# Reordering one pipeline step of a two-stream windowed-attention stage: the first exponentials between the head-out copies, q and k ahead of P on SyncE, and TensorE's third and fourth scores ahead of the second values

## The chip, the cores and the metric

One core of one Trainium2 chip runs the whole program. The time is the device time in microseconds of one execution. The kernel before took 4911.67 us (median of 3 runs, 4908.47 to 4913.42).

## The reference, cut to what matters

The program computes a modulated block: a layer norm, an RWKV-like recurrence over 4096 tokens of two batches, and then two layers of windowed attention with a gated MLP. The change touches only those two layers. With the window length 128, 8 heads of 64, and T = 4096:

```python
def _layer(x, wqkv, qs, ksc, wo, lg, lb, w1, b1, w2, b2):
    h = shift_token(x)
    q, k, v = split(h @ wqkv)                      # 8 heads of 64
    q, k = rotary_xpos(l2norm(q) * qs, l2norm(k) * ksc)
    o = local_attention(q, k, v)                   # own window of 128 keys and the one before
    x = x + o @ wo
    h = layernorm(shift_token(x)) * lg + lb
    a, g = split(h @ w1 + b1)
    return x + (a * gelu(g)) @ w2 + b2

for l in range(2):
    x = _layer(x, ...)
return x_attn + gb * x
```

All tensors are float32.

## The kernel before

Five stages run one after the other: setup, mix, scan, gate and local. `local_stage` holds the two layers. A window is 128 tokens; a layer has NW = 32 windows, and both layers are walked in one loop over u = 0 to 63 (u < 32 is the first layer). Two streams s = 0, 1 are the two batch elements. The work is cut into steps called `half(s, u, w, l)`, with w = u % 2. Such a step does the score and softmax part of stream s, window u, and at the same time the second part (values, output projection, layer norm, MLP) of the other stream o = 1 - s, whose window `um` was scored one step earlier. It also projects q, k and v of the window u + 1 of its own stream s. There are 128 steps; all but the first have the second part (`mlp=True`).

Each engine has its own list of these parts, in an order written out by hand; engines run their lists in order and meet by semaphores. The order on each engine in one step before the change:

- TensorE (PE): values 0 and 1 of o (`values`, L2516, needs group 0 of the turned P), scores 0 and 1 of s (`scores`, L2498, needs the turned q and k), in the second layer the two transposes of `turn_out` (L2567), values 2 and 3 of o (needs group 1 of P), scores 2 and 3 of s, `project_out` of o (L2524, needs both head-out copies), then k projection, mean, v projection, variance, q projection (L2462, L2529, L2533), `hidden` (L2551) and `out` (L2559).
- Scores of head pair 0 and 2 are written to banks B and C of stream s, those of pair 1 and 3 to bank A of s and bank A of o. So scores 2 wait until `row_max` 0 has read its banks, and scores 3 wait until `row_max` 1 has read its own (the wait for `mx` with `after(n, 2)`).
- VectorE (DVE): `add_out`, `norm_k`, `row_max` 0 (L2182: mask and maximum, then L2189: the negative bias `nb`), in the second layer `scale_out`, `row_max` 1, 2, `inverse_sums` 0, `row_max` 3, `attended` (L2206, needs `project_out`), `inverse_sums` 1, `turn_k` (L2156), the four `turn_p` (L2198) with other parts between, and the q work and `gate` of the MLP.
- ScalarE (ACT): `carry`, `head_out` 0 and 1 (L2363: copy of the values' result out of PSUM; number 1 needs values 2 and 3), `exponent` 0 to 3 (L2354, needs `nb` of its pair), `square_dev`, `copy_v`, and the rest.
- GpSimd (POOL): `rotate_k` (L2015 to L2020), `normalise` 0, `join_x1`, `normalise` 1 and 2, and the rest.
- SyncE (SP) moves P and q, k through scratch memory to turn them: `write_p` 0 (L1919), `write_qk` of the other stream (L1898), `write_p` 1, `read_p` 0 (L1931, four transfers), `read_qk` (L1909, four transfers), `read_p` 1. A read waits for the landing of its write. What is read in one step is used by PE in the next.

Of the kernel before, what the change touches and what calls it, by code (L numbers as in the profile page):

```python
# [1745 lines left out]
def local_stage(nc, persist, a, T):  # L1746
# [14 lines left out]
    with ExitStack() as ctx:  # L1761
# [92 lines left out]
        with nc.Block() as block:  # L1854
            @block.sync
            def _(sp):
# [30 lines left out]
                def write_qk(s, u):  # L1887

                    sp.wait_ge(S["q_turned"][s].sem, S["q_turned"][s].after(u))
                    sp.sem_inc(sems["free"], 1)  # L1890
                    sp.wait_ge(S["k_turned"][s].sem, S["k_turned"][s].after(u))
                    sp.sem_inc(sems["free"], 1)
                    sp.wait_ge(S["qkT"][s].sem, S["qkT"][s].after(u, 1))
                    sp.sem_inc(sems["free"], 1)
                    if not isinstance(u, int) or u > 1:
                        sp.wait_ge(S["kT"][s].sem, S["kT"][s].after(u - 1))
                        sp.sem_inc(sems["free"], 1)
                    sp.dma_start(a["qkz"][s], qk[s][:].rearrange("p j y h t -> p (j y h t)")).then_inc(S["qk_out"][s].sem, 16)  # L1898

                def read_qk(s, u, w):  # L1900

                    sp.wait_ge(S["qk_out"][s].sem, S["qk_out"][s].after(u))
                    sp.sem_inc(sems["free"], 1)
                    sp.wait_ge(Q["sc"][s].sem, Q["sc"][s].after(u * NHP - 1))
                    sp.sem_inc(sems["free"], 1)
                    turned = a["qkz"][s].rearrange("(i c) (j n) -> j c i n", i=BL, j=BL)
                    cur = (2, 1)[w] * BL
                    for j in range(BL):
                        sp.dma_start(qkT[s][32 * j:32 * j + 32, cur:cur + BL].rearrange("p i y h t -> p i (y h t)"),  # L1909
                                     turned[j]).then_inc(S["qkT"][s].sem, 16)  # L1910

                def write_p(s, u, g):

                    sp.wait_ge(Q["p_turned"][s].sem, Q["p_turned"][s].after(u * NHP + 2 * g + 1))
                    sp.sem_inc(sems["free"], 1)
                    sp.wait_ge(H[g]["pT"][s].sem, H[g]["pT"][s].after(u, 1))
                    sp.sem_inc(sems["free"], 1)
                    n = 32 * NHP
                    sp.dma_start(bass.AP(a["pz"].tensor, (s * 2 + g) * AREA + (BL - 1) * 32 * n,  # L1919
                                         [[(2 * BL + 1) * n, P], [32 * n, NR], [1, n]]),  # L1920
                                 pb[s][:, g].rearrange("p r h t -> p (r h t)")).then_inc(H[g]["p_out"][s].sem, 16)
# [28 lines left out]
                def half(s, u, w, l, mlp=True):  # L1950
                    o = 1 - s
                    um, wm_ = partner(s, u, w)
                    un, wn = um + 1, 1 - wm_
                    fin = not isinstance(u, int) or u > 0
                    if fin and not layer(u - 1, l):
                        store(s, u - 1, 0)
                    if at(s, u, 1, NW):
                        sp.wait_ge(S["w2_ps"][1].sem, S["w2_ps"][1].after(NW - 1))
                        sp.dma_start(w2[:], a["w2"][1]).then_inc(sems["w2"], 16)
                    if s == 1 and within(u + 2):  # L1960
                        load_rot(u + 2, w, layer(u + 2, l))
                    if mlp and within(um + 2):
                        if isinstance(um, int) and um + 2 == NW:
                            sp.wait_ge(sems["zero"], 16 * NB)
                        load_window(o, um + 2, wm_, layer(um + 2, l))
                    if mlp and layer(um, l):
                        load_xa(o, um)
                    if at(s, u, 0, NW):
                        sp.wait_ge(S["wo_ps"][1].sem, S["wo_ps"][1].after(NW - 1))
                        sp.dma_start(wo[:], a["wo"][1]).then_inc(sems["wo"], 16)  # L1970
                    write_p(s, u, 0)
                    if within(un):
                        write_qk(o, un)
                    write_p(s, u, 1)
                    read_p(s, u, 0)
                    if within(un):
                        read_qk(o, un, wn)
                    read_p(s, u, 1)
                    if fin and layer(u - 1, l):
                        store(s, u - 1, 1)  # L1980
                    if at(s, u, 1, NW - 2):
                        sp.wait_ge(S["q_ps"][1].sem, S["q_ps"][1].after(NW - 1))
                        sp.dma_start(wqkv[:], a["wqkv"][1]).then_inc(sems["wqkv"], 16)
                    if at(s, u, 0, NW):
                        sp.wait_ge(M["w1_ps"][1].sem, M["w1_ps"][1].after(3 * NW - 1))
                        sp.dma_start(w1[:], a["w1s"]).then_inc(sems["w1"], 16)
# [326 lines left out]
            def _(act):  # L2313
# [96 lines left out]
                def half(s, u, w, l, mlp=True):  # L2410
                    o = 1 - s
                    um, wm_ = partner(s, u, w)
                    un, wn = um + 1, 1 - wm_
                    if mlp:
                        carry(o, um, wm_)
                        head_out(o, um, 0)
                        head_out(o, um, 1)
                    exponent(s, u, 0)
                    exponent(s, u, 1)
                    exponent(s, u, 2)  # L2420
                    exponent(s, u, 3)
                    if mlp:
                        square_dev(o, um)
                    if within(un):
                        copy_v(o, un, wn)
                    if within(u + 1):
                        square_k(s, u + 1)
                    if mlp:
                        inverse_std(o, um)
                    if within(u + 1):  # L2430
                        square_q(s, u + 1)
                    if mlp:
                        gelu(o, um, 0, layer(um, l))
                        gelu(o, um, 1, layer(um, l))
                        gelu(o, um, 2, layer(um, l))
                        act.preload_act_table_set(LN_EXP)
                    if within(u + 1):
                        inverse_norms(s, u + 1)
                    if w == 0:
                        copy_k(s, u)  # L2440
# [13 lines left out]
            def _(pe):  # L2454
# [126 lines left out]
                def half(s, u, w, l, mlp=True):  # L2581
                    o = 1 - s
                    um, wm_ = partner(s, u, w)
                    fin = not isinstance(u, int) or u > 0
                    drained = within(um + 1)
                    if mlp:
                        values(o, um, wm_, 0, layer(um, l))
                        values(o, um, wm_, 1, layer(um, l))
                    scores(s, u, w, 0)
                    scores(s, u, w, 1)  # L2590
                    if fin and layer(u - 1, l):
                        turn_out(s, u - 1)
                    if mlp:
                        values(o, um, wm_, 2, layer(um, l))
                        values(o, um, wm_, 3, layer(um, l))
                    scores(s, u, w, 2)
                    scores(s, u, w, 3)
                    if mlp:
                        reloaded("wo", o, um)
                        project_out(o, um)  # L2600
                    if within(u + 1):
                        reloaded("wqkv", s, u + 1)
                        project(s, u + 1, 1 - w, 1)
                    if mlp:
                        mean(o, um)
                    if within(u + 1):
                        project(s, u + 1, 1 - w, 2)
                    if mlp:
                        variance(o, um)
                    if within(u + 1):  # L2610
                        project(s, u + 1, 1 - w, 0)
                    if mlp:
                        reloaded("w1", o, um)
                        hidden(o, um, 0, drained, u)
                        hidden(o, um, 1, drained)
                        hidden(o, um, 2, drained)
                        reloaded("w2", o, um)
                        out(o, um, 0)
                        out(o, um, 1)
                        out(o, um, 2)  # L2620
# [146 lines left out]
```

## Time and profile before

| what | value |
|---|---|
| median of the runs | 4911.67 us |
| the profiled execution | 4915.73 us, its span 4913.9 us |
| PE busy | 4346.3 us (88%) |
| DVE busy | 3295.8 us (67%) |
| ACT busy | 2920.9 us (59%) |
| POOL busy | 2290.3 us (47%) |
| granted TensorE clock, mean | 0.956 |
| local stage | from about 2316 us to the end |
| one step in it | 20.0 us where nothing is late |

An instruction's start is counted from the start of the span. A step begins where PE starts values 0. Groups of matmuls are merged in the rows of the timeline: one row gives the first start and the time until the last one's modelled end. Matmuls overlap, so a group's modelled end lies a little behind the start of the next.

### The profile page before, as it was taken

To read this page: it belongs to the slowest core of one execution; us is meant where nothing else is said; L and a number is where in the kernel's file an instruction comes from. 1 tells how busy PE (TensorE), PEld (TensorE's weight loads), DVE (VectorE), ACT (ScalarE), POOL (GpSimd) and SP (SyncE) were. 2 spreads that over 40 slices of the span, in tenths; PEclk is the share of its full clock that TensorE was granted. 3 is DMA by queue.
4 is the path that set the end of the run, shared out by engine and by line. 5 is a ranking of instruction groups with operands and counts; after the bars stand their busy time and mean duration, and the time that the engine had idled before them with its cause. 6 is when DMAs were issued, how large, how long until landed. Compare 5 with 4: busy or idle time off the path is not lost. (4 is left out here: it accounts for less than half of the span.)

```text
span 4913.9 us, 281580 instructions
## 1 busy us (share of the span) xinstructions
PE 4346.3 (88%) x114072; PEld 3665.2 (75%) x114072; DVE 3295.8 (67%) x10277; ACT 2920.9 (59%) x8550; POOL 2290.3 (47%) x3196
## 2 busy tenths in 40 slices
PE   7888888678888888665999999999999999999998
PEld 6888888668888888653777777777777777777776
DVE  4666666578888888474666666666666666666664
ACT  5777777534444444253666666666666666666665
POOL 1222222257777777302444445444445555555553
PEclk8999999879999999787999999999999999999999
DMA  3334343467777777595666666666676667676665
GB/s 88 88 94 97 90 94 95 103 147 163 164 167 163 164 166 163 143 296 160 153 156 156 154 154 152 151 152 155 162 176 159 160 163 164 161 162 161 158 158 121
DMA packets 1454099, 728.62 MB, mean 148 GB/s; under 512 B 676624, under 2 KB 1398288, under 8 KB 1452816
## 3 DMA queue, kind: packets, MB, share of 16 engines
q1 hardware_dynamic: 1402448, 652.89, 57.6%
q10 hardware_dynamic: 51392, 73.02, 5.1%
q14 instruction: 188, 1.54, 0.1%
q8 instruction: 71, 1.16, 0.1%
HBM read 410.48 MB, written 315.15 MB: 148 GB/s over the span
## 5 line engine op out<-in xcount | busy, mean ns | idle before, releaser
L2354 ACT ACTIVATE l_prob<-l_prob,l_nb,l_rq 128x160 f32<-128x160 f32 x1024 | 518.4, 509 | 14.3 <-DVE l_nb L2189 14.3
L2015 POOL TENSOR_TENSOR l_k<-l_kn,l_tab 128x512 f32<-128x512 f32 x128 | 162.1, 1267 | 613.2 <-DVE l_kn L2163 613.2
L2031 POOL TENSOR_TENSOR l_prob<-l_prob,l_rinv 128x320 f32<-128x320 f32 x512 | 362.8, 719 | 76.3 <-DVE l_rinv L2171 76.1
L2559 PE MATMUL lD<-l_hid,w 128*128 128x128 f32 x3072 | 363.9, 275 | 0.0
L2559 PEld LDWEIGHTS lD<-l_hid,w 128*128 128x128 f32 x3072 | 353.3, 192 | 0.0
L2551 PEld LDWEIGHTS lA<-l_hn,w 128*128 128x128 f32 x2048 | 243.1, 195 | 110.3 <-POOL l_hn L2049 61.1
L2198 DVE STREAM_TRANSPOSE l_pb<-l_prob 128x320 f32<-128x320 f32 x512 | 250.6, 498 | 104.1 <-POOL l_prob L2031 104.1
L2025 POOL TENSOR_TENSOR l_qr<-l_q 128x512 f32<-128x512 f32 x128 | 162.4, 1269 | 329.0 <-DVE l_q L2127 329.0
L1097 POOL TENSOR_TENSOR sc_aqx<-sc_late,sc_headmask 128x256 f32<-128x256 f32 x256 | 172.1, 672 | 278.3 <-PE sc_Y L1190 275.0
L1173 PE MATMUL sc_AB<-sc_aq,sc_bkx 32*32 32x32 f32 x16384 | 258.6, 198 | 39.9 <-POOL sc_bkx L1097 29.7
L497 POOL TENSOR_TENSOR rk<-rk,bkraw 128x256 f32<-128x256 f32 x64 | 54.6, 872 | 477.8 <-DVE bkraw L383 477.8
L2551 PE MATMUL lA<-l_hn,w 128*128 128x128 f32 x2048 | 266.3, 284 | 12.1 <-POOL l_hn L2049 5.6
L2524 PE MATMUL lD<-l_oT,wo 128*128 128x128 f32 x2048 | 264.5, 283 | 0.1
L2524 PEld LDWEIGHTS lD<-l_oT,wo 128*128 128x128 f32 x2048 | 240.1, 193 | 32.7 <-ACT l_oT L2363 30.5
L2462 PE MATMUL lB<-wqkv,l_h 128*128 128x512 f32 x512 | 244.4, 600 | 21.9 <-POOL l_mean_w L2072 21.5
L1115 POOL TENSOR_TENSOR sc_bkT<-sc_tok,sc_headmask 128x128 f32<-128x128 f32 x512 | 257.0, 522 | 0.0
L2551 PE MATMUL lB<-l_hn,w 128*128 128x128 f32 x2048 | 252.0, 277 | 0.0
L1173 PEld LDWEIGHTS sc_AB<-sc_aq,sc_bkx 32*32 32x32 f32 x16384 | 214.5, 108 | 41.9 <-issue 40.9
L2363 ACT COPY l_oT<-lB 128x256 f32<-128x256 f32 x128 | 47.6, 372 | 330.7 <-PE lB L2516 330.7
L2551 PEld LDWEIGHTS lB<-l_hn,w 128*128 128x128 f32 x2048 | 241.7, 194 | 0.0
L2462 PE MATMUL lC<-wqkv,l_h 128*128 128x512 f32 x512 | 241.6, 594 | 0.0
L2462 PE MATMUL lA<-wqkv,l_h 128*128 128x512 f32 x512 | 240.9, 593 | 0.0
(273 smaller groups left out, 13217.1 us busy)
## 6 DMA issues: line engine op xcount, KB each, us to landing
l_pT<-scratch_pz SPq DMA_DIRECT2D x1024, 128.0 KB, 3.7
scratch_pz<-l_pb SPq DMA_DIRECT2D x256, 320.0 KB, 3.0
scratch_qkz<-l_qk SPq DMA_DIRECT2D x128, 512.0 KB, 3.2
l_qkT<-scratch_qkz SPq DMA_DIRECT2D x512, 128.0 KB, 3.8
scratch_cm<-cm SPq DMA_DIRECT2D x64, 512.0 KB, 4.1
sc_early<-scratch_cm ACTq DMA_DIRECT2D x59, 512.0 KB
scratch_tok<-vt SPq DMA_DIRECT2D x512, 48.0 KB, 1.8
scratch_part<-sc_att SPq DMA_DIRECT2D x64, 384.0 KB
```

Of the source, the lines that this page charges most:

```text
L1097: return nc.gpsimd.tensor_tensor(dst[:], src.unsqueeze(2).broadcast_to([P, 2 * BG, HQ, CH]), headmask[:].unsqueeze(1).unsqueeze(3).broadca ...
L1115: last = nc.gpsimd.tensor_tensor(bkT[c % 2][:, b * BG:(b + 1) * BG], tok[k][:, c, b, 1:3].rearrange("p x g i -> p (x g) i").unsqueeze(2) . ...
L1173: last = mm(AB_ps[c][at, (x * BG + q) * QH:(x * BG + q + 1) * QH], bkx[c][at, 2 * q + x].rearrange("p h t -> p (h t)"), aq[c][at, q], star ...
L2015: tt(k1[s][:], kn[s][:], wide(2, slice(0, DH)), ALU.mult)
L2025: tt(qr[s][:], q1[s][:], q2[s][:], ALU.add).then_inc(S["qr"][s].sem, 1)
L2031: tt(prob[s][:, pair], prob[s][:, pair], rinv[s][:, pair].unsqueeze(2).broadcast_to([P, 2, SPAN]), ALU.mult).then_inc(Q["pn"][s].sem, 1)
L2198: nc.vector.transpose(pb[s][:, g, :, at:at + 2].rearrange("p r h t -> p h r t"), prob[s][:, 2 * hp:2 * hp + 2].rearrange("p h (r k) -> p h ...
L2354: last_ = nc.scalar.activation(prob[s][:, h], prob[s][:, h], ACT.Exp, scale=rq8[s][:, h:h + 1], bias=nb[s][:, h:h + 1], accum_out=sums[s][ ...
L2462: last_ = mm(bank[s][j][:], h[:, k * P:(k + 1) * P], wqkv[:, k, j * INNER:(j + 1) * INNER], start=(k == 0), stop=(k == CC - 1))
L2524: last_ = mm(bank[s][3][:, m * P:(m + 1) * P], wo[:, k, m * P:(m + 1) * P], oT[s][:, k], start=(k == 0), stop=(k == NHP - 1))
L2551: last_ = mm(bank[s][j][0:MW, at:at + P], w1[:, k, tile * MW:(tile + 1) * MW], hn[s][:, k], start=(k == 0), stop=(k == CC - 1))
L2559: last_ = mm(bank[s][3][:, c * P:(c + 1) * P], w2[:, m, c * P:(c + 1) * P], hid[s][:, m], start=(c == 0 and m == 0), stop=(c == CC - 1 and ...
```

## The change

Three lists are reordered; nothing is added or removed. On ACT, the first exponentials go between the two head-out copies. On SP, `write_qk` goes ahead of `write_p` 0, and `read_qk` ahead of `read_p` 0. On PE, scores 2 and 3 go ahead of values 2 and 3.

```diff
@@ sync, half
-                    write_p(s, u, 0)
                     if within(un):
                         write_qk(o, un)
+                    write_p(s, u, 0)
                     write_p(s, u, 1)
-                    read_p(s, u, 0)
                     if within(un):
                         read_qk(o, un, wn)
+                    read_p(s, u, 0)
                     read_p(s, u, 1)
@@ scalar, half
                     if mlp:
                         carry(o, um, wm_)
                         head_out(o, um, 0)
+                    exponent(s, u, 0)
+                    if mlp:
                         head_out(o, um, 1)
-                    exponent(s, u, 0)
                     exponent(s, u, 1)
@@ tensor, half
                     scores(s, u, w, 1)
                     if fin and layer(u - 1, l):
                         turn_out(s, u - 1)
+                    scores(s, u, w, 2)
+                    scores(s, u, w, 3)
                     if mlp:
                         values(o, um, wm_, 2, layer(um, l))
                         values(o, um, wm_, 3, layer(um, l))
-                    scores(s, u, w, 2)
-                    scores(s, u, w, 3)
                     if mlp:
                         reloaded("wo", o, um)
                         project_out(o, um)
```

## Rows read from the trace of the kernel before

**Rows 1.** Waits, 3000 to 4800 us (89 steps): who waited, for what, total, times, longest.
```profile
PEld lB L2516 <- DMA l_pT<-scratch_pz: 77.2, 89, 1.7
PEld lD L2524 <- ACT l_oT L2363: 21.1, 84, 0.3
PE lB L2498 <- DMA l_qkT<-scratch_qkz: 16.9, 15, 1.9
```
**Rows 2.** Timeline of PE, a first-layer step: start, length, operation, count [idle before].
```profile
3126.49 1.09 PE L2516 MATMUL lD<-l_pT,l_V 128*64 128x128 f32 x16
3127.82 0.49 PE L2498 MATMUL lA<-l_qkT 64*32 64x160 f32 x16
3129.39 1.09 PE L2516 MATMUL lB<-l_pT,l_V 128*64 128x128 f32 x16 [1.08 <-DMA l_pT<-scratch_pz]
3131.12 2.05 PE L2524 MATMUL lD<-l_oT,wo 128*128 128x128 f32 x16
```
**Rows 3.** Timeline of ACT, the same step: the second head-out copy.
```profile
3130.53 0.37 ACT L2363 COPY l_oT<-lB 128x256 f32<-128x256 f32 x1 [2.52 <-PE lB L2516]
```
**Rows 4.** Windows: stretch, length, busy PE, PEld, DVE, ACT, POOL, clock, DMA, GB/s.
```profile
3131.20:3146.40 15.20, 15.20 (x100) 11.92 (x100) 10.00 (x35) 11.30 (x32) 7.03 (x10) 1.00 0.65 169
3614.00:3617.40 3.40, 1.26 (x40) 0.87 (x42) 1.64 (x13) 0.34 (x1) 3.09 (x4) 1.00 1.10 292
3617.40:3620.80 3.40, 3.40 (x50) 2.48 (x46) 1.37 (x12) 2.20 (x8) 1.28 (x2) 0.50 0.99 392
```
**Rows 5.** Timeline of DVE: turn_k; bias of pair 0 and maximum of pair 1.
```profile
3113.39 0.69 DVE L2156 STREAM_TRANSPOSE l_qk<-l_kr 128x512 f32<-128x512 f32 x1
...
3128.74 0.43 DVE L2189 TENSOR_TENSOR l_nb<-l_mx,l_nrq 128x2 f32<-128x2 f32 x1
...
3129.59 0.08 DVE L2182 DVE_READ_ACCUMULATOR2_ANT l_mx<- 128x1 f32 x1
3129.70 0.16 DVE L2189 TENSOR_TENSOR l_nb<-l_mx,l_nrq 128x2 f32<-128x2 f32 x1
```
**Rows 6.** Timeline of POOL, the same step.
```profile
3127.89 1.27 POOL L2015 TENSOR_TENSOR l_k<-l_kn,l_tab 128x512 f32<-128x512 f32 x1 [5.35 <-DVE l_kn L2163]
```
**Rows 7.** Timeline of 3660.5 to 3664 us: maximum of pair 1, then scores 3.
```profile
3661.35 0.08 DVE L2182 DVE_READ_ACCUMULATOR2_ANT l_mx<- 128x1 f32 x1
...
3661.58 0.51 PE L2498 MATMUL lA<-l_qkT 64*32 64x160 f32 x16
```
**Rows 8.** Timeline of PE, a second-layer step.
```profile
4223.18 0.51 PE L2498 MATMUL lA<-l_qkT 64*32 64x160 f32 x16
4223.61 0.44 PE L2567 MATMUL lD<-ident,l_hout 128*128 128x128 f32 x2
4224.55 1.09 PE L2516 MATMUL lB<-l_pT,l_V 128*64 128x128 f32 x16 [0.49 <-DMA l_pT<-scratch_pz]
```
**Rows 9.** Timeline of DVE, the same second-layer step: maximum of pair 1.
```profile
4225.21 0.08 DVE L2182 DVE_READ_ACCUMULATOR2_ANT l_mx<- 128x1 f32 x1
```
**Rows 10.** Lines L2206 and L2567 over the whole span: durations, first and last start.
```profile
L2206 DVE TENSOR_TENSOR l_x<-lD,l_h x128: 424/425/427, 2327.7 to 4893.7; 128x256 f32<-128x256 f32 x128
L2567 PE MATMUL lD<-ident,l_hout x128: 272/300/331, 3638.9 to 4910.1; 128*128 128x128 f32 x128
```
**Rows 11.** Timeline of SP's queue, a first-layer step.
```profile
3116.66 0.34 SPq L1898 DMA_DIRECT2D scratch_qkz<-l_qk  x1
3117.72 0.36 SPq L1919 DMA_DIRECT2D scratch_pz<-l_pb  x1
3118.72 2.30 SPq L1931 DMA_DIRECT2D l_pT<-scratch_pz  x4
3121.21 1.74 SPq L1909 DMA_DIRECT2D l_qkT<-scratch_qkz  x4
3123.13 1.79 SPq L1931 DMA_DIRECT2D l_pT<-scratch_pz  x4
```
**Rows 12.** Line L1909, 3121.2 to 3123 us: from issue to landing.
```profile
DMA to landing us min/median/max: 3.5/3.9/4.1
```

## The prediction

> **What bounds the kernel now.** I read the page first: the local stage fills the second half of the span, and PE is its busiest engine. The view of waits then says which waits of PE are real. In 89 steps the loads of values 2 wait for the landing of P's group 1 in every one of them, 77.2 us; the output projection waits 0.25 us each for the second head-out copy [rows 1]. The timeline of one step puts these in order. PE starts values 0 at 3126.49, ends scores 1 at 3127.82 + 0.49 = 3128.31, is idle 1.08 us for the DMA, starts values 2 at 3129.39 and the output projection at 3131.12 [rows 2]. That copy starts 1.14 us behind values 2 and takes 0.37 us [rows 3]: 3129.39 + 1.14 + 0.37 = 3130.90, and the projection starts 0.22 us later. So scores 2 and 3 now run in the shadow of that copy and cost nothing. From the projection to the end of the step PE has no gap: 15.20 of 15.20 us busy [rows 4]. The step is therefore one chain: projection, dense PE work, values 0 and 1, scores 0 and 1, a wait, values 2, copy, projection. The wait before values 2 is its only slack of any size, and everything after it moves with the start of values 2.
>
> **PE: scores 2 and 3 ahead of values 2.** The work is the same, but its place is not. Scores 3 overwrite the banks that the maximum of pair 1 reads, so they wait for `row_max` 1, and PE takes its list in order, so values 2, the copy and the projection queue behind that wait. In the first-layer step the maximum of pair 1 ends at 3129.59 + 0.08 = 3129.67 [rows 5]. From such an end to scores 3 the trace of before has one case where PE waited for it: 3661.35 + 0.08 = 3661.43, scores 3 at 3661.58, 0.15 us [rows 7]. From scores of that form to the next work on PE is 4223.61 - 4223.18 = 0.43 us [rows 8]. Values 2 would start at 3129.67 + 0.15 + 0.43 = 3130.25 instead of 3129.39: +0.86 us. The same sum in the second layer, where `scale_out` stands on DVE ahead of `row_max` 1: 4225.21 + 0.08 + 0.15 + 0.43 = 4225.87 instead of 4224.55 [rows 8, 9]: +1.32 us. The neighbouring steps give 0.93 and 1.27 by the same working; I take 0.90 and 1.30.
> Behind values 2 the chain keeps its length: the 1.14 us, the copy and the 0.22 us; only that scores 2 and 3 no longer fill it, which leaves PE idle there about 0.7 us. The shift of values 2 is thus the shift of the step.
> The count: L2206 runs 128 times, once for each second part, the last of them in the closing part, which the change leaves alone: 127 steps. L2567 runs 128 times at two a step, 64, of which two are in the closing part: 62 steps with the longer DVE queue, 65 without [rows 10]. 65 x 0.90 + 62 x 1.30 = 58.5 + 80.6 = 139 us.
>
> Why `row_max` 1 is late has a term of its own. DVE's bias of pair 0 took 0.43 us, the one after it, of the same form, 0.16 [rows 5]; the first ended at 3129.17, where POOL's L2015 ended (3127.89 + 1.27 = 3129.16) [rows 6]. The Trainium skill (SBUF — State Buffer, Who interferes with whom) has the rule for it: a VectorE instruction with two inputs in SBUF and a GpSimd one that reads SBUF exclude each other, and the second to issue blocks for the whole of the first. By the rule the 0.43 stays as long as L2015 starts first; without it the bias would cost 0.16, and the sum would be 127 x 0.27 = 34 us less. The change moves neither instruction against the other, so I keep 0.43, and keep the 34 us as the lower bound of the term.
>
> **ACT: exponentials 0 between the copies.** They can start when the bias of pair 0 is there, 3129.17, and last two activations of 0.51 us by start to start, until about 3130.3. The second copy, then due at 3130.25 + 1.14 = 3131.39, finds ACT free 1.1 us before. Cost 0. They gain 0 too: the exponentials' users, `inverse_sums` 1 and the P turns, stand on DVE behind `attended`, which needs the projection. If values 2 did start at 3129.39 as before, the copy due at 3130.53 would still be clear of them, by 0.2 us.
>
> **SP: q and k first.** `write_qk` needs `turn_k`, done at 3113.39 + 0.69 = 3114.08 [rows 5], and SP is then at the end of the window load that stands before it. It goes out at about 3114.5 instead of 3116.66 [rows 11] and lands before `write_p` 1, so `read_qk` starts at 3118.2, right behind `write_p` 1 (3117.72 + 0.36), where SP now idles until 3118.72 [rows 11]. Then four q, k reads to 3120.0, P's group 0 to about 3122.4, group 1 to 3124.3 instead of 3124.92. What each queue move does:
> - q and k land about 3 us sooner. Scores waited for them in 15 of 89 steps, 16.9 us [rows 1], by 127/89 that is 24 us that can go.
> - P's group 0 is behind them now. Its last read goes out at about 3122.0, where it used to be before 3118.72 + 2.30 = 3121.0, and lands 3.5 to 4.1 us later (the q and k reads in that place have it so [rows 12]): 3125.5 to 3126.1, and values 0 want it at 3126.49 [rows 2]. In a usual step this is in time by 0.4 to 1.0 us. In the 15 of 89 steps where DMAs ran late it is not, and PE will wait at values 0 for what it waited for at scores 0. The two cancel within 0 to 24 us either way; I take 0 and keep -24 and +24.
> - P's group 1 lands 0.6 us sooner, which would be worth 0.6 us a step in the old order. Now values 2 wait for DVE, and this gain is hidden.
>
> **Sum.** 139 + 0 + 0 = 139 us on the profiled execution's 4915.73 (span 4913.9 and 1.8 around it): 5055. That execution is 4.1 above the median, so the median comes to 4911.7 + 139 = 5051.
>
> **The rivals.**
> - A, the forecast: PE's new wait for `row_max` 1. With bounds -34 and -24, +24, about 5000 to 5078.
> - B, faster: the DMA is the loop's real clock. P's group 1 lands 0.6 to 0.9 us sooner and scores 2 and 3 fill the time until then, so the step shortens by up to 0.6: 127 x 0.6 = 76 us, 4835. For it: the DMA wait stands in all 89 steps. Against: scores 3 must be out before the landing, that is, the maximum of pair 1 must end by 3129.39 - 0.6 - 0.43 - 0.15 = 3128.2, and it ends at 3129.67, 1.5 us late. It decides for B only if DVE reaches that maximum before 3128.2.
> - C, P's group 0 becomes late: the reads of 0.4 us slack slip to a wait at values 0 in most steps, 0.4 us each: 139 + 51 = 190 us, 5102. For it: the slack is thin. Against: the whole burst starts 0.5 us earlier.
> - D, absorbed: some slack between projection and values 0 swallows part of the shift; half of it would give 4912 + 70 = 4982. Against: the 15.20 of 15.20 us [rows 4].
> - E, the clock: at 3614.0 to 3617.4 PE was busy 1.26 of 3.40 us and the clock granted in the next 3.4 us was 0.50 (1.2 GHz) [rows 4]. With the new order a step has three idle pieces close together, 0.5, 0.5 and 0.7 us, but some 2.1 of 3.4 us stay busy. A stretch of 3.4 us at half the clock loses 1.7 us at most; in one step of three that is 42 x 1.7 = 71 us on top of A: 5122. The Trainium skill (TensorE: Matmul & The Clock Gate, A second HAM failure mode: psum-queue depth-cycling) says that a TensorE which idles briefly and often between groups of matmuls, as it cycles through PSUM banks, can swing between its two clocks. By that rule this new order is a candidate for E; the trace shows such a fall only once in the steady stage, after much more idling, and speaks against it.
>
> **How the numbers follow.** A 0.77, B 0.05, C 0.09, D 0.05, E 0.04. The predicted time is A's, 5051. Range 5005 to 5095: A without its lowest corner, and the near part of C. A measurement of this kernel tells 0.2%, about 10 us, from no change. Faster is B, 0.05; the same is the far end of D, 0.02; slower the rest, 0.93.
>
> **What would show it.** Right: in the profile after, the DMA wait before values 2 is gone; scores 3 start 0.15 us behind the maximum of pair 1; values 2 start some 3.8 us behind values 0 in the first layer and 4.1 in the second (2.90 before in the first); the projection waits 0.6 to 0.7 us for the copy; steps last 20.9 and 21.3 us. q and k landings no longer appear as waits of scores. Wrong: a DMA wait still ahead of values 2 (B), a wait of L2516's lD loads for P in most steps (C), steps of 20.0 us with idle moved elsewhere (D), granted clock below 1.00 inside the local stage (E).

## The result and the profile after

The changed kernel took 5024.31 us (median of 4 runs, 5023.56 to 5029.4) against 4910.07 us (4 runs): a ratio of 1.0235, 95% interval 1.0218 to 1.0251, about 115 us slower. Forecast were 5051 us, in a range of 5005 to 5095, and slower with 0.93. The profiled span grew from 4913.9 to 5021.7 us.

The waits of the changed kernel, 3000 to 4800 us, about 85 steps (columns as in rows 1). TensorE's lines have moved by one: values are L2517, scores L2499, the projection L2525.
```profile
PE lA L2499 <- DVE l_mx L2182: 55.1, 85, 1.2
PE lB L2499 <- DVE l_mx L2182: 23.7, 69, 0.6
PEld lD L2525 <- ACT l_oT L2363: 59.9, 84, 0.7
PE lD L2525 <- ACT l_oT L2363: 40.2, 85, 0.6
PE lD L2517 <- DMA l_pT<-scratch_pz: 8.5, 12, 1.9
```
The wait of values 2 for P is gone. In [rows 1] their weight loads waited for it in 89 of 89 steps, 77.2 us; as idle time of PE the same view of before has less:
```profile
PE lB L2516 <- DMA l_pT<-scratch_pz: 53.4, 82, 1.3
```
In the changed kernel scores 2 (the lB row) and scores 3 (lA) wait for VectorE's maxima, and the projection (L2525) waits for the copy, now as an idle PE and not only as a held weight load. Values 0 (the lD row of L2517) wait for P in 12 steps, which they did not before; scores no longer wait for q and k at all.

PE in a first-layer step of the changed kernel:
```profile
3193.23 1.09 PE L2517 MATMUL lD<-l_pT,l_V 128*64 128x128 f32 x16
3194.62 0.51 PE L2499 MATMUL lA<-l_qkT 64*32 64x160 f32 x16
3196.55 0.51 PE L2499 MATMUL lA<-l_qkT 64*32 64x160 f32 x16 [0.46 <-DVE l_mx L2182]
3196.99 1.09 PE L2517 MATMUL lB<-l_pT,l_V 128*64 128x128 f32 x16
3198.56 2.05 PE L2525 MATMUL lD<-l_oT,wo 128*128 128x128 f32 x16 [0.47 <-ACT l_oT L2363]
```
VectorE in that step, the bias of pair 0 and the end of the maximum of pair 1, and ScalarE's second copy:
```profile
3195.47 0.44 DVE L2189 TENSOR_TENSOR l_nb<-l_mx,l_nrq 128x2 f32<-128x2 f32 x1
...
3196.33 0.08 DVE L2182 DVE_READ_ACCUMULATOR2_ANT l_mx<- 128x1 f32 x1
```
```profile
3198.13 0.37 ACT L2363 COPY l_oT<-lB 128x256 f32<-128x256 f32 x1 [1.07 <-PE lB L2517]
```
The maximum of pair 1 ends at 3196.41, scores 3 start 0.14 us later, values 2 0.44 us after that: 3.76 us behind values 0, where [rows 2] had 2.90. The copy starts 1.14 us behind values 2, as in [rows 3], and ends at 3198.50; the projection starts at 3198.56, 1.57 us behind values 2, where it was 1.73 before.

The same on PE in a second-layer step:
```profile
4209.19 1.09 PE L2517 MATMUL lD<-l_pT,l_V 128*64 128x128 f32 x16
...
4212.85 0.51 PE L2499 MATMUL lA<-l_qkT 64*32 64x160 f32 x16 [0.80 <-DVE l_mx L2182]
4213.29 1.09 PE L2517 MATMUL lB<-l_pT,l_V 128*64 128x128 f32 x16
4214.85 2.05 PE L2525 MATMUL lD<-l_oT,wo 128*128 128x128 f32 x16 [0.47 <-ACT l_oT L2363]
```
Values 2 stand 4.10 us behind values 0. The rest of the step is as dense as in [rows 4]:
```profile
3198.80:3213.50 14.70, 14.70 (x97) 11.41 (x97) 8.39 (x23) 9.98 (x27) 6.13 (x9) 1.00 0.75 178
```
SP's queue in that step, against [rows 11]: `write_qk` (L1898) is first, the two `write_p` are merged in one row, and the eight P reads in another, behind the q and k reads.
```profile
3202.36 0.35 SPq L1898 DMA_DIRECT2D scratch_qkz<-l_qk  x1
3203.59 2.16 SPq L1919 DMA_DIRECT2D scratch_pz<-l_pb  x2
3206.10 1.79 SPq L1909 DMA_DIRECT2D l_qkT<-scratch_qkz  x4
3208.07 3.76 SPq L1931 DMA_DIRECT2D l_pT<-scratch_pz  x8
```
To compare steps I give the mean starts of three groups behind the start of values 0, and the mean length of a step, in us, over some 57 steps of each layer (first/second), taken from the first matmul of each group in the traces. In a step where nothing is late scores 0 start at 1.02.

| kernel | scores 0 | values 2 | projection | step |
|---|---|---|---|---|
| before | 1.23 / 1.23 | 2.93 / 2.89 | 4.66 / 4.63 | 20.15 / 20.13 |
| changed | 1.02 / 1.02 | 3.75 / 4.07 | 5.32 / 5.63 | 20.90 / 21.23 |

### The profile page after: what moved, and what is told of

It reads as the page before. It is cut to its first block and busy times, and to the rows that moved or that the text cites. A ratio compares the mean times of both kernels' runs of the same rounds, so it can differ in the third digit from the quotient of the medians.

```text
span 5021.7 us, 281580 instructions
## 1 busy us (share of the span) xinstructions
PE 4380.2 (87%) x114072; PEld 3659.5 (73%) x114072; DVE 3322.9 (66%) x10277; ACT 2936.8 (58%) x8550; POOL 2292.5 (46%) x3196
## 5 line engine op out<-in xcount | busy, mean ns | idle before, releaser
L2525 PE MATMUL lD<-l_oT,wo 128*128 128x128 f32 x2048 | 262.6, 281 | 60.1 <-ACT l_oT L2363 60.0
L2525 PEld LDWEIGHTS lD<-l_oT,wo 128*128 128x128 f32 x2048 | 238.2, 191 | 91.0 <-ACT l_oT L2363 90.2
L2189 DVE TENSOR_TENSOR l_nb<-l_mx,l_nrq 128x2 f32<-128x2 f32 x512 | 207.2, 405 | 17.9
```

The lines of the kernel that those rows point to most:

```text
L2189: tt(nb[s][:, pair], mx[s][:, pair], nrq8[s][:, pair], ALU.mult).then_inc(Q["nb"][s].sem, 1)
L2525: last_ = mm(bank[s][3][:, m * P:(m + 1) * P], wo[:, k, m * P:(m + 1) * P], oT[s][:, k], start=(k == 0), stop=(k == NHP - 1))
```

## The experiments

Theory W: the loss is PE's in-order wait for the maximum of pair 1, in front of values 2, the copy and the projection. Theory D: SP's order costs, as P's group 0 comes late behind q and k; this is rival C of the prediction, and not its D. Theory X: the exponentials of pair 0 hold up the second copy. A second question is why that maximum is late.

### Each list alone: pe_only, sp_only, act_only

`pe_only` has the diff's third part alone, `sp_only` the first, `act_only` the second.

> Only TensorE's list is reordered. Theory W (TensorE's new wait for the maximum of pair 1 makes the change slower): values 2 start 3.76 and 4.10 us behind values 0 as in the changed kernel, so the loss is all here: +115 to +135 us, a ratio of 1.024 to 1.027. It should be a little above the whole change, because the late landings of q and k (0.2 us a step before) stay. Theory D (SyncE's order costs: P's group 0 lands late behind q and k): at most half of the 115 us is here, a ratio under 1.012. Theory X (the exponentials ahead of the second copy hold up the projection): the same, under 1.012.

> Only SyncE's list is reordered. Theory W: in the old order of TensorE the start of values 2 is the landing of P's group 1, and that landing now comes 0.75 us sooner, counted from attended, as the changed kernel's trace has it (15.4 against 16.1 us). The step loses the wait, 0.5 to 0.9 us in the first layer and 0.4 to 0.7 in the second, 127 steps: -60 to -105 us, a ratio of 0.979 to 0.988. Theory D: P's group 0 makes values 0 wait, by 0.1 to 0.9 us a step, and the kernel is slower or at best the same, 1.000 to 1.02.

> Only ScalarE's list is reordered. Theory W: the exponentials of pair 0 end 0.1 to 0.3 us before the second copy is due, no effect: a ratio of 0.999 to 1.001. Theory X: the copy waits for them in each step, by at most the 1.2 us that they last; with half of that 76 us, 1.015.

| kernel | median us | ratio to before, 95% |
|---|---|---|
| pe_only | 5054.56 | 1.0296 (1.0282 to 1.031) |
| sp_only | 4841.05 | 0.9856 (0.9841 to 0.9872) |
| act_only | 4916.53 | 1.0008 (0.9999 to 1.0017) |

Each goes W's way. PE's reorder alone costs 145 us, more than the whole change and 10 us above the upper end of what I expected. SP's reorder alone gains 71 us: theory D is wrong in sign. ScalarE's alone is nothing that can be told from 0. One step of `sp_only` on PE:
```profile
3211.04 1.09 PE L2516 MATMUL lD<-l_pT,l_V 128*64 128x128 f32 x16
3212.43 0.51 PE L2498 MATMUL lA<-l_qkT 64*32 64x160 f32 x16
3213.10 1.09 PE L2516 MATMUL lB<-l_pT,l_V 128*64 128x128 f32 x16 [0.16 <-DMA l_pT<-scratch_pz]
3214.42 0.48 PE L2498 MATMUL lA<-l_qkT 64*32 64x160 f32 x16
3214.83 2.05 PE L2524 MATMUL lD<-l_oT,wo 128*128 128x128 f32 x16
```
The 1.08 us of waiting in [rows 2] are 0.16: P's group 1 really lands earlier, values 2 start at 2.06, and a step takes 19.48 us in the first layer and 19.82 in the second, on average.
In `pe_only` the late landings of q and k stay, as they should:
```profile
PE lB L2498 <- DMA l_qkT<-scratch_qkz: 14.6, 13, 1.7
PE lA L2498 <- DVE l_mx L2182: 53.4, 84, 1.1
```
In the old order a late start of scores was partly swallowed by the wait for P (values 2 late by 0.09 us on average where scores 0 were late by 0.21); here it passes on whole, so that values 2 start at 3.96 us on average in the first layer, not 3.75. Also its granted clock was 0.50 in five stretches between 2350 and 4960 us, 27.3 us together; the changed kernel had none there (each kernel has a few at the start and the end of the local stage).

### The change less one part: sp_act, pe_act, pe_sp

> The whole change without its TensorE part. Theory W: as sp_only where the copy is not held up. With values 2 starting 0.7 us sooner the copy is due at about 3.2 us behind values 0, and the exponentials of pair 0, which cannot start before 2.7, last until about 3.9: here they should cost, by 0.5 us a step, up to 64 us against sp_only: a ratio of 0.988 to 1.000. If the copy is not held up, the ratio is that of sp_only. Theory D: 1.00 to 1.02.

> The change without its SyncE part. Theory W: in the changed kernel the early q and k take away the late landings at scores 0 (0.2 us a step before) and bring a wait for P's group 0 at values 0 (0.08 us): without the SyncE part the kernel is 5 to 20 us slower than the whole change, ratio 1.025 to 1.028, and values 2 still start behind scores 3, not at a landing. Theory D: it is faster than the whole change by 10 us or more, since values 0 no longer wait: under 1.021.

> The change without its ScalarE part. Theory W: the exponentials end 0.7 us or more before the second copy is due, so they cost nothing, and early exponentials gain nothing since their users stand behind attended: as the whole change, ratio 1.022 to 1.025. Theory X: faster than the whole change by 10 us or more, under 1.021.

| kernel | left out | median us | ratio to before, 95% |
|---|---|---|---|
| sp_act | PE's part | 4864.51 | 0.9908 (0.9893 to 0.9923) |
| pe_act | SP's part | 5061.26 | 1.0315 (1.0295 to 1.0336) |
| pe_sp | ScalarE's part | 5029.07 | 1.0245 (1.0231 to 1.0259) |

Without PE's part the change would have been a gain. Beside PE's new order SP's part is worth 25 us from pe_only to pe_sp (1.0296 to 1.0245) and 39 us from pe_act to the whole change (1.0315 to 1.0235), against 71 us in the old order. pe_act lies above what I expected (1.025 to 1.028). Its trace shows late landings (scores 0 at 1.22 on average) and four stretches at clock 0.50 beyond 2350 us, 23.9 us together, but the traced execution, 5050.95 us, is the fastest of its five, 10 us below their median; what lengthened the others is not shown. Theory X fails beside PE's new order: `pe_sp` is not faster than the whole change. But it is right in `sp_act`, by 25 us against `sp_only` by the medians (0.9856 to 0.9908), as expected from where the exponentials end. The second copy in `sp_act`, and the wait before it in `act_only`, 3000 to 4800 us:
```profile
3207.06 0.35 ACT L2363 COPY l_oT<-lB 128x256 f32<-128x256 f32 x1
```
```profile
ACT l_oT L2363 <- PE lB L2517: 7.7, 19, 1.4
```
In `sp_act` ScalarE goes from the exponentials into the copy with no idle time between, and the projection stands at 4.14 us in both layers whatever values 2 do (2.10 and 2.24 us on average). In `sp_only` it stands at 3.89 and 4.14: the cost shows in the first layer alone, 65 x 0.25 = 16 us, near the 14 us between the two traced executions (4845.71 and 4859.90 us). In `act_only`, with values 2 later, the two ends nearly meet: ScalarE still waited for PE in 19 of 89 steps, and scores 2 and 3 in front of the projection cover the rest.

### Scores 2 ahead, scores 3 not: s2_first

```diff
                     scores(s, u, w, 2)
-                    scores(s, u, w, 3)
                     if mlp:
                         values(o, um, wm_, 2, layer(um, l))
                         values(o, um, wm_, 3, layer(um, l))
+                    scores(s, u, w, 3)
```


> The whole change, but scores 3 stay behind values 3; only scores 2 go ahead of values 2. They wait for the maximum of pair 0 (end 2.21 us behind values 0) and not for that of pair 1 (3.17 and 3.51). Theory W: scores 2 start at 2.36, values 2 at 2.79 in both layers, against 3.76 and 4.10 in the changed kernel and 2.94 and 2.89 before: the loss is gone, ratio 0.990 to 1.000, if the exponentials do not hold the copy (due at 3.93, their end at 3.9). Theory D: the loss stays, 1.01 or more.

The kernel took 4889.37 us, 0.9952 (0.9939 to 0.9966). Values 2 start at 2.80 us in both layers, the expected 2.79 within 0.01. One call of `scores`, with its wait for `row_max` 1, is the difference between 0.5% faster and 2.4% slower. It is still 0.0044 behind `sp_act`, which differs from it in PE's order alone: even scores 2 wait for a maximum that ends after P's landing. The 0.0096 to `sp_only` holds ScalarE's part as well.

### What makes the maximum of pair 1 late: max_first, k1_between

`max_first` changes VectorE's order in the whole change. Cut to the order of the calls (the bias is taken out of `row_max` into a function of its own, and the two maxima get separate scratch cells):
```diff
-                    row_max(s, u, w, 0)
+                    row_max(s, u, w, 0, with_bias=False)
+                    row_max(s, u, w, 1, with_bias=False)
+                    bias(s, u, 0)
                     if fin and lp:
                         scale_out(s, u - 1)
-                    row_max(s, u, w, 1)
+                    bias(s, u, 1)
```


> The whole change, and on VectorE the maximum of pair 1 goes ahead of the bias of pair 0 and of scale_out; the two write separate one-column scratch cells. The work is the same. Theory W: the maximum of pair 1 ends at about 2.8 us behind values 0 in both layers instead of 3.17 and 3.51, values 2 start at 3.4 instead of 3.76 and 4.10: 65 x 0.38 + 62 x 0.72 = 69 us less than the whole change, ratio 1.007 to 1.013. Theories D and X: no difference to the whole change, 1.022 to 1.025, or slower, since the exponentials of pair 0 get their bias later.

The kernel took 4948.47 us, 1.0079 (1.0065 to 1.0092). The maximum ends at 2.71 us in both layers, scores 3 start at 2.86, values 2 at 3.30, steps last 20.44 and 20.48 us: 0.46 and 0.75 us less than in the changed kernel. 76 us of the 115 were thus the bias of pair 0 and `scale_out` in front of that maximum. The other 39 us stay: with the maximum at 2.71 values 2 still start at 3.30, where the landing of P let them start at 2.93 and 2.89 before.

`k1_between` changes GpSimd's order in the whole change:
```diff
-                    tt(k1[s][:], kn[s][:], wide(2, slice(0, DH)), ALU.mult)
                     tt(k2[s][:, :, lo], kn[s][:, :, hi], wide(3, lo), ALU.mult)
+                    tt(k1[s][:], kn[s][:], wide(2, slice(0, DH)), ALU.mult)
```


> The whole change, and on GpSimd the 512-element product of rotate_k (1.27 us) stands between the two 256-element ones (0.73 us each) instead of ahead of them; the same work. The bias of pair 0 on VectorE is issued 2.2 us behind values 0. Theory P (the bias, with two inputs in SBUF, is blocked until the GpSimd instruction that runs then ends): that instruction now ends at 3.4 instead of 2.67, the bias takes 1.1 instead of 0.43 us, and the maximum of pair 1, scores 3, values 2 and the step come 0.7 us later: 127 x 0.7 = 89 us, ratio 1.040 to 1.043. Rival (the 0.43 us are VectorE's own): no change, 1.022 to 1.025.

The kernel took 5158.39 us, 1.0506 (1.0491 to 1.052): further than expected. First the bias of pair 0, then GpSimd in the same step:
```profile
3217.25 1.11 DVE L2189 TENSOR_TENSOR l_nb<-l_mx,l_nrq 128x2 f32<-128x2 f32 x1
```
```profile
3217.07 1.27 POOL L2016 TENSOR_TENSOR l_k<-l_kn,l_tab 128x512 f32<-128x512 f32 x1
```
The bias ends at 3218.36, 0.02 us behind GpSimd's product (3218.34): 1.11 us for an operation of the form that took 0.16 in [rows 5]. That is no single case. Of the 512 biases in this trace 310 took more than 0.18 us, and each of them ended 0.01 to 0.03 us behind the GpSimd instruction that ran when it began; the 76 that met none took 0.16. In the kernel before, the same holds for 380 of 382, and 43 of 43 took 0.16. The Trainium skill describes this exclusion (SBUF — State Buffer, Who interferes with whom), and the trace agrees to 0.02 us.

The median shift of values 2 against the changed kernel is 0.68 us in both layers, the 0.7 expected. On average a step that kept its full clock is 0.53 us longer in the first layer and 0.56 in the second, 69 us over 127 steps; that is less than 0.68 a step, since in some steps the bias ends sooner. The rest, some 65 of the 133 us, is the clock, rival E of the prediction. Windows in this kernel (columns as in rows 4):
```profile
2995.90:2999.30 3.40, 1.72 (x70) 0.88 (x56) 2.97 (x18) 1.31 (x5) 3.25 (x4) 1.00 0.14 39
2999.30:3002.70 3.40, 2.94 (x23) 2.53 (x20) 1.53 (x8) 1.88 (x8) 1.38 (x2) 0.50 0.00 0
3002.70:3006.10 3.40, 3.40 (x18) 2.29 (x18) 1.71 (x6) 1.51 (x7) 1.58 (x3) 1.00 0.00 0
```
After 1.72 us busy of 3.40 the granted clock was 0.50, 1.2 GHz, for the next 3.4 us. The trace has 38 stretches at 0.50 in the local stage before its last steps, 146.8 us; in the 3.4 us ahead of each PE was busy 1.60 to 1.82 us. Of 116 steps compared, the 36 that hold such a stretch are longer than the others of their layer by 1.58 us (21 steps) and 1.87 us (15 steps), 61 us, or by 127/116 some 67 us. With the 69 us that makes 136, against 133 by the ratio. The Trainium skill (TensorE: Matmul & The Clock Gate, A second HAM failure mode: psum-queue depth-cycling) describes a clock that swings when TensorE idles briefly and often between groups of matmuls while it cycles through PSUM banks. The trace agrees: the idle pieces before scores 2 and 3 are waits for PSUM banks that VectorE still reads, and in the changed kernel, whose wait before scores 3 is 0.7 us shorter in most steps, the clock did not fall there.

### Where SP's gain comes from, and a faster version: write_first, sp_max

`write_first` has only `write_qk` moved; the reads keep their old order. `sp_max` is `sp_only` with the VectorE order of `max_first`.

> Of SyncE's edit only the early write_qk; the reads keep the order P group 0, q and k, P group 1. Reads can start only when P's group 0 has landed in scratch, 5.7 us behind attended, and not at 5.3 when SyncE is free. If the gain of SyncE's order is the early write (its 512 KB out of the burst of reads), this keeps most of it: ratio 0.985 to 0.990. If the gain is that the q and k reads fill SyncE's idle time before P's landing, 0.5 to 0.7 us of issue time, most of it goes: 0.993 to 1.000. Theory D, for the small wait at values 0: it goes, P's group 0 lands 2 us ahead.

> SyncE's new order alone, and on VectorE the maximum of pair 1 ahead of the bias of pair 0 and of scale_out; TensorE and ScalarE as before. With SyncE's order alone the projection starts 0.41 us behind the start of scores 3, and in the second layer these wait for the maximum of pair 1 (3.51, scores 3 at 3.66, against 3.41 in the first). Theory W: that maximum ends at 2.71 us, as in max_first, scores 3 stand right behind scores 2 in both layers, and 62 steps gain 0.1 to 0.25 us: 6 to 15 us less than SyncE's order alone, ratio 0.982 to 0.985. Rival: the step is bound by the landing of P there, no difference, 0.9856 within 0.001.

`write_first`: 4861.13 us, 0.9905 (0.989 to 0.992). `sp_max`: 4834.76 us, 0.9845 (0.9831 to 0.9858). Moving the 512 KB write is most of the gain, 47 of 71 us; the order of the reads gives the rest. That lies between the two ranges I had set (0.985 to 0.990, and 0.993 to 1.000), next to the first. SP in `write_first`:
```profile
3204.63 2.16 SPq L1919 DMA_DIRECT2D scratch_pz<-l_pb  x2
3207.99 1.80 SPq L1931 DMA_DIRECT2D l_pT<-scratch_pz  x4
3210.05 1.73 SPq L1909 DMA_DIRECT2D l_qkT<-scratch_qkz  x4
3211.97 1.78 SPq L1931 DMA_DIRECT2D l_pT<-scratch_pz  x4
```
Between the second write and the first read SP waits 1.2 us for P's landing (3206.79 to 3207.99); in the changed kernel the q and k reads start 0.35 us behind it (3205.75 to 3206.10). P's group 0 then lands 2.7 us ahead of values 0 on average in the first layer, where it is 0.4 us in the changed kernel, and values 0 do not wait for it at all. So the wait at values 0 is the price of the read order, and a small one. The wait of PE before values 2 is 38.8 us in the 1800 us, where it was 53.4 before and is 16.5 in `sp_only`.
`sp_max` is the fastest kernel of the study, 1.5% ahead of before. Its lead over `sp_only` is 0.0011, within both intervals; the traces show the second-layer step at 19.68 instead of 19.82 us, the part that was expected, but by time alone it is not shown.

## Why the prediction was right, and by how much it was off

The direction, the place and the mechanism were right, and the signs I named are in the trace. One of them has the wrong size: I said that the projection waits 0.6 to 0.7 us for the copy; its weight loads wait 0.71 us, but PE is idle for 0.47. The forecast of 139 us was 24 us above the 115 measured, from terms that missed by 13, 21 and 11 us, the last the other way. Step by step:

- **Scores 3 wait for `row_max` 1.** Right to 0.05 us: values 2 at 3.76 and 4.10 us against the 3.8 and 4.1 stated. `s2_first` and `max_first` move exactly that wait and move the time with it.
- **The baseline of the shift was off.** I took the shift in undisturbed steps, 0.90 and 1.30 us, 139 us. In the mean of all steps values 2 stood at 2.93 and 2.89 before, some of them late by a late landing; against that the shifts are 0.82 and 1.18 us: 65 x 0.82 + 62 x 1.18 = 126 us.
- **"Behind values 2 the chain keeps its length."** This failed, by 0.17 us a step, 21 us. I read PEld's wait for the copy [rows 1] as what set the projection. But the projection's matmuls stood behind scores 2 and 3 (in [rows 2] they start 1.73 us behind values 2, with the copy ended at 1.51); once both are out of the way they start 0.06 us behind the copy's end. Scores 2 and 3 were not wholly in the shadow; they cost these 0.17 us, and the change gave them back. `s2_first` bears this out: with scores 3 alone in between, the projection also stands 1.57 us behind values 2.
- **SP, taken at 0 with 24 us either way.** Beside PE's new order it gives 25 us by one pair of kernels and 39 us by the other, at the edge of the bound and beyond it. Both halves are in the trace: the late q and k landings went (scores 0 at 1.02 instead of 1.23 us), and values 0 now wait for P's group 0 in some steps, 0.09 us on average, 11 us. The first two points already hold what the landings gave.
- **SP's gain hidden behind PE's new wait.** Right, and of the size I priced: 71 us in `sp_only`, which keeps PE's old order, where 0.6 us a step made 76. B, the same gain with PE's new order, did not come: its condition (the maximum by 3128.2) was not met.
- **ScalarE at 0.** Right here. It is not free in general: once P comes earlier it costs 25 us by the medians (`sp_act` against `sp_only`).
- **The 0.27 us of the bias.** Kept as measured, and `k1_between` shows why it is there.
- **The bounds of A.** 139 with -34 and -24 gives 4993, with +24 it gives 5075; "5000 to 5078" is a little off at both ends. The range and the forecast do not hang on it.

126 - 21 + 11 = 116 us, against 115 by the ratio and 108 by the two profiled spans. C is there at 0.09 us a step instead of 0.4. The prediction's D did not occur. Nor did E: from 2318 to 4963 us the granted clock of the changed kernel is 1.00.

## What to carry to other kernels

Before work is moved ahead of a wait, look for the waits that the moved work brings with it, and compare when each ends: here a wait for a DMA that ended at 2.8 us was replaced by one for another engine that ended at 3.2 to 3.5. Parts of a reorder should be timed alone, for a good one (SP's, 1.4% faster) can sit unseen under a bad one. And a wait shown on a weight load is not an idle PE: what sets a matmul's start is the later of its operand and the matmuls in front of it.

## What the runs showed of the hardware

- VectorE's 128x2 product of two SBUF operands, 0.16 us alone, took 1.11 us behind a GpSimd product of 1.27 us, to the end of that product. So its time goes by what GpSimd still has to do, not by its own size. Putting the longer GpSimd instruction in its way cost the kernel, with what followed, 2.7% (1.0235 to 1.0506).
- In `k1_between` the granted clock fell to 0.50 (1.2 GHz) 38 times in the local stage before its last steps, each time with PE busy 1.60 to 1.82 us in the 3.4 us ahead; PE was idle there 97.9 + 23.3 + 38.2 = 159 us before the maxima and the copy in 1800 us. The changed kernel, with 55.1 + 23.7 + 40.2 = 119 us of such idle time, had no fall between 2318 and 4963 us.
- Issuing one 512 KB write some 1.6 us earlier, ahead of the other writes and the reads, brought the kernel 1% (`write_first`). In the kernel before, the DMA engines were busy for the whole of the stretch in which it lay (share 1.00, 3116.6 to 3126.5 us). That the gain comes from less traffic in that stretch fits this, but is not shown by a run of its own.
